# Raw feature rows fetched in two parts per tile, and three other forms of the same gather, in a one-core graph-network layer

## What is computed

```python
h = jnp.maximum(_layernorm(x, axis=-1), 0.0)
w = relu(edge_attr_10 @ W_fc1 * ...) @ W_fc2 * ...      # 192 weights per edge
l0, l1 = h0 @ W_l1_0 * a * ..., einsum(h1, W_l1_1) * a  # one row of 160 per node: the table
y0, y1 = l0[edge_src], l1[edge_src]                     # gather by source node
m0, m1, m2, m3 = products of w, y and edge_attr_4
s0..s3 = segment_sum(m, edge_dst)                       # scatter by target node
out = x + (h @ W_si) * a + 0.5 * (s @ W_l2) * a / FAN_L2
```

## Time and profile before

| | before |
|---|---|
| median of 2 runs | 3994.18 us |
| the profiled execution | 3994.23 us |
| its span | 3990.3 us |
| POOL busy | 2996.3 us, 75% |
| PE busy | 3419.6 us, 86% |
| DVE busy | 2055.0 us, 51% |
| ACT busy | 1071.0 us, 27% |
| gathers of table rows (L839) | 3083, 945 ns each |
| gathers of raw rows (L278) | 84, 972 ns each |
| mean granted TensorE clock | 0.819 |

### The profile page before, as it was taken

The page is one execution under the profiler, slowest core; times in us unless marked ns, Lnnn a source line. Parts: engine busy times, 40 slices in busy tenths (PEclk is TensorE's granted clock), DMA queues, the critical chain, the costliest instruction groups (busy, mean ns, idle before and its releaser), DMA issues.

```text
span 3990.3 us, 79986 instructions
## 1 busy us (share of the span) xinstructions
PE 3419.6 (86%) x17464; PEld 1994.6 (50%) x17464; DVE 2055.0 (51%) x7424; ACT 1071.0 (27%) x2487; POOL 2996.3 (75%) x3171
## 2 busy tenths in 40 slices
PE   6788888888888888888888888888988888888888
PEld 5444545455544545455545554555545454445544
DVE  7454555455445555545555555555555554545554
ACT  5222222222222222222222222222222222222222
POOL 6777777777777777777777777777777777777776
PEclk8788888788778888778887888878788787878877
DMA  9555555555555555556555555555555555555554
GB/s 318 143 146 143 136 151 138 146 146 138 137 143 141 140 146 137 137 143 149 140 146 136 147 138 144 140 144 141 143 145 136 146 141 146 137 145 138 146 144 120
DMA packets 732079, 582.48 MB, mean 146 GB/s; under 512 B 397562, under 2 KB 655438, under 8 KB 731214
## 3 DMA queue, kind: packets, MB, share of 16 engines
q1 hardware_dynamic: 568800, 308.24, 28.6%
q0 software_dynamic: 152016, 259.69, 27.2%
q10 hardware_dynamic: 10782, 9.37, 0.8%
HBM read 421.88 MB, written 155.04 MB: 145 GB/s over the span
## 4 chain that ended last, share of the span: by engine, by line
POOL 43%; DMA 18%; issue 16%; PE 15%; DVE 8%; ACTq 0%; ACT 0%; SPq 0%; DVEq 0%; POOLq 0%
POOL R L839 42%; DMA R<-l_table,src 17%; DVE R L1082 5%; PE bank L658 4%; PE bank L1161 4%; DVE R L1079 3%; PE bank L1174 2%; PE bank L1151 2%; POOL ZD L278 1%; PE bank L701 1%; DMA raw_rows<-ZD 0%; ACTq L1010 0%; PE bank L681 0%; DMA x<-in_xp 0%; PE bank L409 0%
## 5 line engine op out<-in xcount | busy, mean ns | idle before, releaser
L839 POOL DMA_INDIRECT R<-l_table,src x3083 | 2914.5, 945 | 939.9 <-issue 822.2
L1079 DVE TENSOR_TENSOR R<-bank,R 128x256 f32<-128x256 f32 x1584 | 668.9, 422 | 1809.9 <-DMA R<-l_table,src 1199.7
L1161 PE MATMUL bank<-w,hs 100*128 100x192 f32 x6446 | 1495.5, 380 | 90.3 <-DVE R L1082 83.8
L1161 PEld LDWEIGHTS bank<-w,hs 100*128 100x128 f32 x6446 | 1248.4, 223 | 473.8 <-issue 438.0
L1174 PE MATMUL bank<-R 128*32 128x320 f32 x6448 | 714.6, 519 | 392.7 <-DVE R L1082 387.0
L1082 DVE TENSOR_TENSOR R<-bank,R 128x192 f32<-128x192 f32 x3168 | 967.3, 347 | 0.0
L951 ACT ACTIVATE E<-bank 128x320 f32<-128x320 f32 x806 | 352.3, 437 | 2244.3 <-PE bank L1174 1496.2
L1151 PE MATMUL bank<-ea,w1s 10*100 10x512 f32 x1612 | 543.9, 756 | 8.4 <-DMA ea<-in_ea_p 7.6
L945 ACT ACTIVATE hs<-bank 100x512 f32<-100x512 f32 x806 | 435.9, 594 | 272.8 <-PE bank L1151 272.4
L1174 PEld LDWEIGHTS bank<-R 128*32 128x32 f32 x6448 | 147.8, 116 | 626.7 <-issue 625.6
L658 PE MATMUL bank<-ZD 128*128 128x448 f32 x776 | 424.7, 704 | 5.1 <-issue 5.1
(11 more groups left out here) (111 smaller groups left out, 855.1 us busy)
## 6 DMA issues: line engine op xcount, KB each, us to landing
s_tiles<-E SPq DMA_DIRECT2D x806, 160.0 KB
lone_act<-l_table ACTq DMA_DIRECT2D x4096, 0.6 KB
R<-l_table,src POOLq DMA_INDIRECT x3083
ea<-in_ea_p SPq DMA_DIRECT2D x403, 96.0 KB
ZD<-s_tiles SPq DMA_DIRECT2D x392, 96.0 KB, 2.4
ZD<-s_tiles SPq DMA_DIRECT2D x97, 320.0 KB
psc<-l_table SPq DMA_DIRECT2D x1536, 0.6 KB
H<-l_table SPq DMA_DIRECT2D x1536, 0.6 KB
```

The costliest lines, as they stand in the source:

```text
L839: PL.indirect_dma_start(out=Y[:, g % NB, t, :], out_offset=None, in_=T, in_offset=bass.IndirectOffsetOnAxis(ap=src[:, k:k + 1], axis=0),). ...
L1079: V.tensor_tensor(p[:, :, :, 0:64], w[:, :, 0:128].rearrange("p t (s c) -> p t s c", s=2), y[:, :, 0:64].unsqueeze(2).to_broadcast([128, n ...
L1161: m = PE.matmul(b[:, o * 192:(o + 1) * 192], hs[:, g % 4, t * 128:(t + 1) * 128], w2[:, :], start=True, stop=True, skip_group_check=True)
```

## The change

Nothing is changed in what the gathers bring, where they put it, or in the main stage. What changes is the form of the gathers for the 21 raw quads, by r modulo 7:

- remainder 0, 1, 2, 3 (three quads each, 12 in all): each tile is fetched in two gathers, the first of 122, 124, 113 or 112 rows, the second of the remaining 6, 4, 15 or 16
- remainder 4: one gather per tile, source and destination seen as int32
- remainder 5: one gather per tile, with a bound check on the indices
- remainder 6: one gather per tile, source and destination seen as int16 (322 elements in a row)

The second parts have index columns of their own that start at partition 0, so `src_raw` grows from 84 to 132 columns. `raw_store` waits for the larger count of arrivals (`arrived`).

```diff
+def cuts(r):
+
+    cut = {0: 122, 1: 124, 2: 113, 3: 112}.get(r % 7, 128)
+    return ((0, cut), (cut, 128)) if cut < 128 else ((0, 128),)
+
+def cut_columns(n):
+
+    out = []
+    for r in range(n):
+        for t in range(G):
+            for i, (p, e) in enumerate(cuts(r)):
+                out.append((r, t, i, p, e))
+    return out
...
-        src_raw = sb("src_raw", [128, max(NR, 1) * G], i32)
+        CUT = cut_columns(NR)
+        ncut = [0] * NRB
+        arrived = []
+        for r in range(NR):
+            ncut[r % NRB] += 16 * G * len(cuts(r))
+            arrived.append(ncut[r % NRB])
+        src_raw = sb("src_raw", [128, max(len(CUT), 1)], i32)
...
-            for t in range(G):
-                k = r * G + t
-                PL.indirect_dma_start(
-                    out=ring[:, r % NRB, t, :], out_offset=None, in_=a["xa"],
-                    in_offset=bass.IndirectOffsetOnAxis(ap=src_raw[:, k:k + 1], axis=0),
-                ).then_inc(s_rg[r % NRB], 16)
+            for k, (rr, t, i, p, e) in enumerate(CUT):
+                if rr != r:
+                    continue
+                where = bass.IndirectOffsetOnAxis(ap=src_raw[0:e - p, k:k + 1], axis=0)
+                if r % 7 == 4:
+                    PL.indirect_dma_start(out=ring[p:e, r % NRB, t, :].bitcast(i32), out_offset=None,
+                                          in_=a["xa"].bitcast(i32), in_offset=where).then_inc(s_rg[r % NRB], 16)
+                elif r % 7 == 5:
+                    PL.indirect_dma_start(out=ring[p:e, r % NRB, t, :], out_offset=None, in_=a["xa"],
+                                          in_offset=where, bounds_check=NP - 1).then_inc(s_rg[r % NRB], 16)
+                elif r % 7 == 6:
+                    PL.indirect_dma_start(out=ring[p:e, r % NRB, t, :].bitcast(mybir.dt.int16), out_offset=None,
+                                          in_=a["xa"].bitcast(mybir.dt.int16), in_offset=where
+                                          ).then_inc(s_rg[r % NRB], 16)
+                else:
+                    PL.indirect_dma_start(out=ring[p:e, r % NRB, t, :], out_offset=None, in_=a["xa"],
+                                          in_offset=where).then_inc(s_rg[r % NRB], 16)
...
-            SP.wait_ge(s_rg[r % NRB], 64 * (r // NRB + 1))
+            SP.wait_ge(s_rg[r % NRB], arrived[r])
```

More of the change, by code:

```diff
@@ L1426, in lay_out @@
     RAW = raws(n_nodes, n_edges)
-    src_raw = np.zeros((max(len(RAW), 1) * G, 128), np.int32)
-    for r, (k, g) in enumerate(RAW):
-        src_raw[r * G:(r + 1) * G] = src.reshape(-1, 128)[g * G:(g + 1) * G]
+    CUT = cut_columns(len(RAW))
+    src_raw = np.zeros((max(len(CUT), 1), 128), np.int32)
+    for c, (r, t, i, p, e) in enumerate(CUT):
+        src_raw[c, 0:e - p] = src.reshape(-1, 128)[RAW[r][1] * G + t, p:e]
     ROW = single(n_nodes, n_edges)
```

## The result

| | before | after |
|---|---|---|
| median | 3994.18 us (2 runs) | 4076.36 us (2 runs, 4073.68 and 4079.03) |
| ratio | | 1.0207, interval 1.0182 to 1.0232 |
| the profiled execution, its span | 3994.23, 3990.3 us | 4079.03, 4075.2 us |
| first gather of table rows | 116.01 us | 198.24 us |
| gathers of raw rows | 84, busy 81.7 us | 132, busy 154.8 us |

The slowdown is clear of the noise; whether it is over 2% isn't, since the interval is 1.82% to 2.32%.

The account below looks back on a forecast made before the run. POOL's gathers at a fixed beat of 1.250 us were taken as the bound. Extra gathers +50.9 and the vanished wait -5.7 gave +45.2: 3994.2 + 45.2 = 4039.4 us, range 4010 to 4078.

Parts of the forecast that it names:

- The frame: Whole span: POOL gathers table rows every 1.250 us without a stall, so each microsecond its main stage starts later lengthens the end.
- f + v x n / 128: Price of a raw gather of n rows on POOL, f = 1.06 fixed, f + v = 1.250; 48 extra gathers: +50.9 us.
- the second rival: Raw gathers: 113 rows through a single DMA engine hold POOL up, +30 and 4070 us; chance 0.21, 0.10 above 4074.
- the last sentence of the prediction: Raw gathers: the prediction is wrong if a part costs more than a whole gather; no size given.
- the forecast's own mechanism: Raw gathers on POOL: f from 0.8 to 1.25 and nothing held up, 4027 to 4049 us; chance 0.62.
- The fixed part: Each raw gather on POOL: f, the price that doesn't depend on its rows, taken as 1.06 us.
- The wait of 6 us: POOL before quad 10, waiting for quad 3's store to `raw_rows`: goes because POOL arrives later, -5.7 us.
- Views and check: 36 raw gathers as int32, int16 or with a bound check: taken as 0, +18 us at most.
- SP's queue: SP's stores before the main stage: table complete at about 145, POOL through at 161, so 16 us cover it.

## Why the prediction came out as it did

- **The frame was right.** POOL's beat sets the time, the main stage is as long as before, and what POOL loses in the first stage appears at the end: 82.2 us of 84.9.
- **The step that failed is the price of the extra gathers, "f + v x n / 128".** It made a pair cost the same wherever the cut lay, and bounded 48 of them by +60.0. They cost +87.1. The bound above was none: the term excluded that a part could cost more than the whole. That case stood only with the second rival, at 0.21, and in the last sentence of the prediction. So the time came out above the band of the forecast's own mechanism (4027 to 4049), and that it still lies in the stated range, by 1.6 us, is owed to the share of that rival; it is luck more than insight. What stands in the place of n / 128 is rows / k. The fixed part was nearly right: 0.86 + 0.305 = 1.16 for a gather of 16 rows against my 1.06, and the cuts at multiples of 16 came to +50 in all, against the forecast's +45.
- **The wait of 6 us went**, -5.7 as forecast. That it would go by POOL's lateness alone was luck to a part: with few cuts and an early one of 113 rows it stayed.
- **Views and check**: taken as 0, measured 0.8.
- **SP's queue**: the table's last store was issued at 177.94 and those stores take 6.1 us at the median, so it was there at about 184, 14 us before POOL wanted it; forecast 16.
- **The second rival had the right signs and the wrong work.** It said that 113 rows on one engine make POOL slower, by 30 us, to 4070, because POOL waits for room. The gathers that it pointed at are the dear ones. But they cost this before their first row moves and with a seventh of the bytes, and those of 122 and 124 rows, which it left out, are dearer too: (1.69 + 1.29 - 2 x 0.94) x 12 = 13 us. Its time for the rows themselves was too long as well: the estimate of 43 ns for each row gave 4.84 us for 113 rows on one engine, and those of quad 16 took 3.2 to 4.0. The rule of the Trainium skill on the number of engines, which stood beside it, would have given the order of the four cuts had I read it as a price for POOL and not only for the transfer. The size of that price, 13.3 ns for each of rows / k, stood in no row of before.
- **The other rule of the Trainium skill**, "DMA: Bandwidth & Descriptors", in the anatomy of one DMA, that many descriptors can be emitted before their cost shows, nearly holds where the rows spread: 1 and 8 rows for each of 16 take 0.86 and 0.946 us. It doesn't hold for 113 rows with k = 1, which cost 1.5 us more than one row.

## What to carry to other kernels

Count the gathers, and keep the rows of each at a multiple of 16: one more row, 113 instead of 112, made a gather of this kernel take GpSimd two and a half times as long. Where an engine works at a fixed beat, any instruction it gets more is paid in full, and any one it loses is a gain only as long as the queue that takes the work over has room. An upper bound from "a part costs no more than the whole" is a belief about the mechanism; look for what the size decides besides the amount.

## What the runs showed of the hardware

- A gather of 128 rows takes POOL 0.946 us and a pause of 0.305; 16 rows still take 0.86. So some nine tenths of the beat of 1.25 us are there with an eighth of the rows.
- Duration against rows / k: 1 0.88 to 0.90 (2, 4, 6, 9, 15 rows), 8 0.98 (104), 9 0.99 (126), 17 1.08 to 1.10 (34, 119), 19 1.10 to 1.12 (19, 95), 31 1.29 (124), 47 1.48 (94), 61 1.69 (122), 109 2.31 (109), 113 2.38 (113), in us: some 13.3 ns for each of rows / k. A seventh of the bytes changes nothing in it.
- The packets show the same k in the transfer: 124 rows go over four engines, 122 over two, and 113 one after another, 3.2 to 4.0 us for a gather, beginning 1.1 to 2.6 us after POOL has ended it.
- A bound check on the indices adds 0.07 us to a gather; a view as int32 adds nothing, one as int16 0.01 to 0.02.
- Four gathers of 113 rows in the 15 us when other loads fill the DMA engines held up SP's queue: its first raw store slipped from 28.4 to 41.0 us. With that quad cut in 64 + 64 it stood at 27.4.
